# Two head groups of attention values share one PSUM bank, in a one-core transformer layer

## The reference

```
q, k, v = x @ Wq, x @ Wk, x @ Wv              # 16 heads of 8 dimensions; rotary on q and k
attn = softmax(causal(q @ k.T / sqrt(8)))
x = layernorm(x + (attn @ v) @ Wo)
logits = x @ router_w.T + experts_bias        # 8 experts, the best two of a row, softmax of the two
x = layernorm(x + sum_e cw[e] * ffn_e(x) + shared_ffn(x))   # ffn: (silu(x w1) * (x w3)) w2, hidden 256
```

## Time and profile before

| what | us |
|---|---|
| median of 3 runs | 580.99 |
| lowest and highest | 580.41, 583.55 |
| the profiled execution, from first to last instruction | 604.0 |
| TensorE busy in it | 530.3 (88%) |
| VectorE busy | 487.5 (81%) |
| ScalarE busy | 314.4 (52%) |
| GpSimd busy | 309.0 (51%) |

### The profile page before, as it was taken

The page is one execution under the profiler, slowest core; times in us unless marked ns, Lnnn a source line. Parts: engine busy times, 40 slices in busy tenths (PEclk is TensorE's granted clock), DMA queues, the critical chain, the costliest instruction groups (busy, mean ns, idle before and its releaser), DMA issues.

```text
span 604.0 us, 14723 instructions
## 1 busy us (share of the span) xinstructions
PE 530.3 (88%) x4350; PEld 350.6 (58%) x4350; DVE 487.5 (81%) x1981; ACT 314.4 (52%) x744; POOL 309.0 (51%) x517
## 2 busy tenths in 40 slices
PE   6868997988999999999999999999994997999941
PEld 3312354534665656656666777666873996885531
DVE  4797799978999899899899879879951766768883
ACT  3107665646766566667676555776660444532200
POOL 5216546566364466657873556547584324143531
PEclk9777799989999989999999799999997999999985
DMA  6573321265426256454674374643464499960111
GB/s 187 143 238 100 107 81 47 88 207 170 117 73 194 82 155 179 116 165 111 195 188 123 92 237 146 187 129 111 121 186 163 121 283 269 310 219 19 52 40 35
DMA packets 75279, 87.40 MB, mean 145 GB/s; under 512 B 9984, under 2 KB 57984, under 8 KB 75200
## 3 DMA queue, kind: packets, MB, share of 16 engines
q1 hardware_dynamic: 67824, 77.21, 43.5%
q0 software_dynamic: 3584, 7.35, 4.0%
q10 hardware_dynamic: 3792, 1.90, 1.1%
HBM read 64.28 MB, written 20.05 MB: 140 GB/s over the span
## 4 chain that ended last, share of the span: by engine, by line
PE 54%; DVE 14%; issue 9%; SPq 6%; DMA 5%; ACT 4%; another core or an unknown queue 4%; POOL 2%; ACTq 0%; DVEq 0%; POOLq 0%
PE ps L1459 14%; PE ps L1365 9%; PE ps L1321 9%; PE ps L1471 7%; DVE sums L1578 3%; PE ps L1376 3%; ACT probs L1166 2%; PE ps L1443 2%; PE ps L1481 1%; DVE acc L1758 1%; DMA stack<-mparts 1%; SPq L957 1%; POOL yg L1122 1%; PE ps L1307 1%
## 5 line engine op out<-in xcount | busy, mean ns | idle before, releaser
L1578 DVE CUSTOM_DVE_ANT_0 sums<-ps,mask_sb 128x384 bf16<-128x384 f32 (+3 forms) x512 | 218.2, 484 | 18.1 <-PE ps L1321 17.7
L1166 ACT ACTIVATE probs<-ps 128x512 f32<-128x512 f32 x320 | 170.8, 611 | 48.0 <-PE ps L1321 42.5
L1100 POOL TENSOR_SCALAR_AFFINE_SELECT probs<-probs 128x256 f32<-128x256 f32 (+1 forms) x320 | 113.6, 365 | 128.4 <-ACT probs L1166 121.1
L1321 PE MATMUL ps<-stack 64*128 64x256 bf16 (+3 forms) x1024 | 116.6, 311 | 14.6 <-DMA stack<-mparts 5.1
L1459 PE MATMUL ps<-xgT,w_tile 128*128 128x128 f32 x672 | 91.8, 283 | 3.9 <-ACT xgT L1227 1.6
L1459 PEld LDWEIGHTS ps<-xgT,w_tile 128*128 128x128 f32 x672 | 82.7, 195 | 10.5 <-issue 7.6
L1365 PE MATMUL ps<-probs,va 128*32 128x512 f32 (+3 forms) x1024 | 82.6, 466 | 3.3 <-POOL probs L1100 1.7
L1710 DVE SCALAR_TENSOR_TENSOR gate<-th,ps 128x256 f32<-128x256 f32 x116 | 48.5, 418 | 43.0 <-ACT th L1233 36.9
L1321 PEld LDWEIGHTS ps<-stack 64*128 64x128 bf16 x1024 | 41.4, 95 | 70.5 <-issue 16.1
L1122 POOL DMA_INDIRECT yg<-rows_out,slot x56 | 54.0, 963 | 55.0 <-DVE acc L1758 29.9
L1233 ACT ACTIVATE th<-ps 128x256 f32<-128x256 f32 x116 | 45.3, 391 | 48.4 <-PE ps L1459 38.6
(11 more groups left out here) (119 smaller groups left out, 702.5 us busy)
## 6 DMA issues: line engine op xcount, KB each, us to landing
w_tile<-in_experts SPq DMA_DIRECT2D x92, 384.0 KB
stack<-parts_scratch SPq DMA_DIRECT2D x98, 128.0 KB
parts_scratch<-parts SPq DMA_DIRECT2D x14, 384.0 KB
xg<-rows_in SPq DMA_DIRECT2D x18, 256.0 KB
rows_out<-y_routed SPq DMA_DIRECT2D x61, 64.0 KB
rows_in<-zeros SPq DMA_DIRECT2D x14, 192.0 KB, 3.9
x_t<-in_x SPq DMA_DIRECT2D x8, 256.0 KB, 3.6
x_r<-in_x SPq DMA_DIRECT2D x8, 256.0 KB
```

The source lines that it names most:

```text
L1100: pool.affine_select(out=area, in_=area, compare_op=ALU.is_ge, fill=0.0, base=0, pattern=pattern, channel_multiplier=-1).then_inc(masked, 1)
L1166: act.activation(probs[:, (s * NB + v) % PRING, :], bank("scores", s, v), ACT.Exp, scale=SCALE)\
L1321: return pe.matmul(into[:, at:at + width], here[:, stationary, at_s:at_s + P], here[:, moving, at_m:at_m + width], start=True, stop=True)
L1578: ins = dve.tensor_tensor_reduce(sums[:, use % 2, at:at + w], bank("max", s, u)[:, at:at + w], mask_sb[:, S - w:S], -1.0, 3.0e38, ALU.add, ...
```

## The change

- The value groups 0 and 1 accumulate into one bank, and so do 2 and 3. The stationary operand `va` now holds for each pair of heads 48 columns: head one in columns 0 to 8, zeros, head two in columns 32 to 40, zeros. The first group's matmuls read columns 0 to 31, the second's columns 16 to 47, so that in the 32 output rows of a slot head one lands in rows 0 to 8 and head two in rows 16 to 24. The accumulation is started by the first group and ended by the second. The number and the shapes of the value matmuls stay.
- ScalarE copies two banks of a sequence into `ot` instead of four; two transpositions for a row tile instead of four; the results of two row tiles fit one bank, so a call of `heads_transposes` claims one bank instead of two.
- `normalize` does one reciprocal of 32 columns and one product of 256 columns for a call, instead of two of each with half the columns.
- The first group of a pair signals a semaphore of its own (`values_read`), on which the exponentials that reuse its `probs` units wait; the columns of Wv and the rows of Wo are permuted on the host.
- `COST` of the two `heads_T` pieces is changed, a kind `values_out` is added for ACT, and all of `LATER` is replaced.

```diff
-    pe=dict(... heads_T=(890, 1060),
+    pe=dict(... heads_T=(450, 620),
-    dve=dict(... heads_T=(803, 910),
+    dve=dict(... heads_T=(560, 660),
+        for h in range(GROUPS // 2):
+            add(now + AT["values"] + UPG * (2 * h + 2), "values_out", s, h)
+        if kind == "values":
+            both = (key[0], key[1] // 2)
+            return [] if key[1] % 2 else [((kind, *both), (engine, reader, *both))]
-        if kind in ("project", "heads_T", "dense_gate"):
+        if kind in ("project", "dense_gate"):
...
+        def weighed(s, g):
+            return filled("values", s, g // 2) if g % 2 else (values_read, GROUPS // 2 * s + g // 2 + 1)
...
-            pool.memset(va[:, :, :, DK:DK + 1], 1.0).then_inc(setup_p, 1)
+            for side in range(2):
+                ins = pool.memset(va[:, :, :, 32 * side + DK:32 * side + DK + 1], 1.0)
+            ins.then_inc(setup_p, 1)
...
-            def values_out(s, g):
-                act.wait_ge(*filled("values", s, g))
-                if g == 0 and s > 0:
-                    act.wait_ge(*filled("heads_T", s - 1, 1, 1))
-                act.activation(ot[:, g, :], bank("values", s, g), ACT.Copy).then_inc(free("values", s, g), 1)
+            def values_out(s, h):
+                act.wait_ge(*filled("values", s, h))
+                if h == 0 and s > 0:
+                    act.wait_ge(*filled("heads_T", s - 1, 1))
+                act.activation(ot[:, h, :], bank("values", s, h), ACT.Copy).then_inc(free("values", s, h), 1)
...
-                take("values", s, g)
+                into, second = bank("values", s, g // 2), g % 2
+                if not second:
+                    take("values", s, g // 2)
...
-                        last = pe.matmul(bank("values", s, g)[32 * k:32 * k + 32, j * P:S], va[:, j, PER_PV * g + k, :],
-                                         probs[:, (s * NB + v) % PRING, at:at + S - j * P], start=(j == 0), stop=(j == T - 1),
-                                         skip_group_check=True)
-                last.then_inc(full("values", s, g), 1)
+                        last = pe.matmul(into[32 * k:32 * k + 32, j * P:S],
+                                         va[:, j, PER_PV * (g // 2) + k, 16 * second:16 * second + 32],
+                                         probs[:, (s * NB + v) % PRING, at:at + S - j * P],
+                                         start=(j == 0 and not second), stop=(j == T - 1 and second == 1), skip_group_check=True)
+                last.then_inc(full("values", s, g // 2) if second else values_read, 1)
...
+                take("heads_T", s, pair)
                 for n in range(2):
                     t = 2 * pair + n
-                    take("heads_T", s, pair, n)
-                    for g in range(GROUPS):
-                        last = pe.transpose(bank("heads_T", s, pair, n)[:, g * P:(g + 1) * P], ot[:, g, t * P:(t + 1) * P], ident_sb[:, :])
-                    last.then_inc(full("heads_T", s, pair, n), 1)
+                    for h in range(GROUPS // 2):
+                        at = (2 * n + h) * P
+                        last = pe.transpose(bank("heads_T", s, pair)[:, at:at + P], ot[:, h, t * P:(t + 1) * P], ident_sb[:, :])
+                last.then_inc(full("heads_T", s, pair), 1)
...
+                dve.wait_ge(*filled("heads_T", s, pair))
+                oq = bank("heads_T", s, pair).rearrange("p (u c) -> p u c", c=16)
+                inverse = rden[:, 2 * pair:2 * pair + 2, :].rearrange("p t h -> p (t h)")
+                link(dve.reciprocal(inverse, oq[:, :, DK]), rden_done, 2 * s + pair + 1)
+                dve.tensor_tensor(on[:, 2 * pair:2 * pair + 2, :].rearrange("p t (h d) -> p (t h) d", d=DK), oq[:, :, 0:DK],
+                                  inverse.rearrange("p (u o) -> p u o", o=1).broadcast_to([P, 2 * H, DK]),
+                                  ALU.mult).then_inc(free("heads_T", s, pair), 1)
```

Of `LATER` two of its 79 entries, before and after:

```diff
-         ("act", "values"): (-268.17, -117.23, -81.25, 129.78, -56.72, -170.37, -619.73, -885.2, -558.27, -432.32,
-         -110.15, -277.99),
+         ("act", "values_out"): (-2105.76, -1787.93, -1697.56, -583.3, -3888.91, -4689.17, -4349.28, -3516.7, -4293.05,
+         -3093.81, -2874.72, -2037.86),
-         ("pe", "heads_T"): (-709.01, -718.43, -476.07, -268.98, -111.31, -392.14, -837.02, -647.44, -498.38, -598.34,
-         -471.24, -468.92),
+         ("pe", "heads_T"): (-1263.31, -3006.95, -367.24, -2843.55, -1026.06, -1809.9, -3302.95, -2934.64, -1691.2,
+         -763.6, -1651.08, -1775.85),
```

More of the change, by code:

```diff
@@ L422, in build_block @@
               "count": ("dve", "count"), "rank": ("dve", "rank"), "gate": ("dve", "glu"), "project": ("dve", "project"),
-              "heads_T": ("dve", "heads_T"), "score_pair": ("act", "scores"), "max_pair": ("dve", "max"),
+              "heads_T": ("dve", "heads_T"), "values": ("act", "values_out"), "score_pair": ("act", "scores"), "max_pair": ("dve", "max"),
               "dense_gate": ("dve", "dense_glu"), "dense_down": ("dve", "mix"), "dense_end": ("dve", "mix_end")}
@@ L493, in needs @@
             if kind == "heads_T":
-                return [("act", "values", s, GROUPS - 1), ("pe", "out_T", s - 1, 0), ("pe", "heads_T", s, 0) if key[1] else None]
+                return [("act", "values_out", s, GROUPS // 2 - 1), ("pe", "out_T", s - 1, 0), ("pe", "heads_T", s, 0) if key[1] else None]
             if kind == "out_T":
@@ L547, in needs @@
                 return [("dve", "router", s, 0)]
+            if kind == "values_out":
+                return [("pe", "values", s, 2 * key[1] + 1)] + ([("pe", "heads_T", s - 1, 1)] if key[1] == 0 else [])
             if kind == "tanh":
@@ L1193, in store_v @@
                 if s > 0:
-                    act.wait_ge(*filled("values", s - 1, GROUPS - 1))
+                    act.wait_ge(*weighed(s - 1, GROUPS - 1))
                 else:
@@ L1271, in _ @@
                     store_v(key[0])
-                elif kind == "values":
+                elif kind == "values_out":
                     values_out(*key)
@@ L1594, in normalize @@
             def normalize(s, pair):
-                for n in range(2):
-                    dve.wait_ge(*filled("heads_T", s, pair, n))
-                    oq = bank("heads_T", s, pair, n).rearrange("p (h c) -> p h c", c=32)
-                    ins = dve.reciprocal(rden[:, 2 * pair + n, :], oq[:, :, DK])
-                link(ins, rden_done, 2 * s + pair + 1)
-                for n in range(2):
-                    t = 2 * pair + n
-                    oq = bank("heads_T", s, pair, n).rearrange("p (h c) -> p h c", c=32)
-                    dve.tensor_tensor(on[:, t, :].rearrange("p (h d) -> p h d", d=DK), oq[:, :, 0:DK],
-                                      rden[:, t, :].rearrange("p (h o) -> p h o", o=1).broadcast_to([P, H, DK]),
-                                      ALU.mult).then_inc(free("heads_T", s, pair, n), 1)
+                dve.wait_ge(*filled("heads_T", s, pair))
[5 more added lines that the diff above has]
+                                  ALU.mult).then_inc(free("heads_T", s, pair), 1)
             def layernorm_stats(n, rows, src, st, m, ve, chain, var_sem):
```

314 lines of the change are left out of this document (163 added, 151 removed).

## The result

The change made the kernel slower: 592.88 us median (587.70 to 595.64, 4 runs) against 580.85 us (580.41 to 583.55, 4 runs), ratio 1.0185 with a 95% interval of 1.0138 to 1.0231, that is +10.7 us (8.0 to 13.4). I had said 573.0, range 561 to 588. One run of e12, in the chip's slower state, is left out of its ratio.

What follows compares the result with a forecast made beforehand. The prediction took TensorE as the bound from 50 to 450 us, VectorE second. Its terms, -6.9 - 0.4 + 2.2 - 2.9 = -8.0 us, took the median from 580.99 to 573.0 us, range 561 to 588.

Steps and rivals of the forecast that it cites:

- What bounds the kernel: From 150 to 450 us TensorE is 97% busy, VectorE 89%; TensorE's time counts nearly in full, VectorE's in part.
- Transpositions, -6.9: On TensorE, 64 fewer transpositions of the heads at 0.107 us each save 6.9 us.
- Value matmuls and copies, 0: Value matmuls keep number and shapes; 16 fewer ScalarE copies free 9.6 us of busy time; both taken as 0.
- VectorE, -0.4: Normalization saves 2.9 us of VectorE's busy time, worth 0.4 us by its 14% share of the chain.
- Banks, +2.2: Value banks held longer raise TensorE's 4.5 us of waits for VectorE's bank releases by half, costing 2.2 us.
- The rival: Held value banks make score and maxima pairs wait: +12.3 us, 586.0; chance 0.17, shared with an order opening idle time.
- The new order, -2.9: New queue order closes an eighth of TensorE's 23.0 us idle between 50 and 450 us, saving 2.9 us.
- The signs I had named: Trace marks: 64 transpositions, 16 copies, VectorE's two groups near 11.5 us, TensorE busy near 523 us, middle stage shorter.
- TensorE under 95% in the middle: TensorE's busy share from 150 to 450 us falling below 95%, as the sign that the gain is hidden.
- a hidden gain: Rival: VectorE's row maxima set the pace and TensorE only waits more; 581.5 us, range 578 to 584, chance 0.17.
- Idle before the score matmuls released by VectorE of well over 4.5 us: TensorE's idle time before score and maxima matmuls, ended by VectorE's release, as the sign of held banks.

Runs made afterwards that it cites:

- e12: Kernel before with each reciprocal and product of VectorE's normalization issued once more, into an unused tile; 590.40 us, ratio 1.0131.
- e8: Kernel before with each of the 128 transpositions of the heads issued twice; 595.25 us, ratio 1.0190.
- e1: Kernel before, unchanged, run again for a second trace; ratio 1.0000, span 582.4 us.
- e10: The changed kernel, run again against the kernel before; 595.98 us, ratio 1.0214.
- e5: Kernel before, same order; only the planner's bank dealing changed, reserving each even value group's bank until the odd group's copy; 599.60 us, ratio 1.0270.
- e4: Kernel before with ScalarE's copy of each even value group moved right ahead of the odd group's copy; 599.34 us, ratio 1.0266.
- e7: Kernel before in its own order, with seven of the eight PSUM banks in use throughout; 611.05 us, ratio 1.0448.
- e2: Changed kernel with every queue in the order of the kernel before, banks dealt out anew; 593.26 us, ratio 1.0164.
- e3: Kernel before with every queue in the changed kernel's order, two copies where that has one; 596.61 us, ratio 1.0244.
- e9: Changed from kernel before: each value group keeps its own bank, VectorE adds odd to even groups before half as many transpositions; 582.53 us, ratio 1.0002.

## Why the prediction was wrong

*What bounds the kernel.* Right for TensorE, too low for VectorE. Its share of the chain, 14%, was read as the worth of its time. Per us of busy time e12 gives 0.84, at the place that the change touches, with the later results in it. A chain names one engine at each moment, also where two are nearly level, as at the 97% and 89% of the middle stage.

*Transpositions, -6.9.* Right mechanism, size a little over: 5.6 (4.3 to 6.8) by e8. A record takes 277 ns in e1 and 281 ns after. e8 shows that this duration isn't the price, which is a third of it. The Trainium skill (TensorE: Matmul & The Clock Gate, Part 4: PE-mode transpose) gives about 275 ns for one in one kernel's context. As a duration the traces agree with that.

*Value matmuls and copies, 0.* Mean 453 ns against 466 before, but 469 in e10, so nothing is seen. Copies weren't isolated. The 9.1 us for which TensorE waited for the last of them belonged to the untypical execution, as said above.

*VectorE, -0.4.* The two groups are at 12.4 us against 15.0 and 14.7 in e1, so 2.3 us less busy time, not 2.9: the reciprocal of 32 columns takes 353 ns, where I took 290. At 0.84, taken from the same place, it is worth -1.9.

*Banks, +2.2. This is the step that failed.* Measured, the hold costs +15.8 us (e5, interval 12.8 to 18.8) and +15.5 (e4). The step has +2.2 us and the runs show 15.8 in its place. The mechanism, its place and its length (21.6 us more in the sequence of the earlier trace rows) were right. The rival had priced it at 12.3 and put the outcome at 586.0, with its range up to 596; the change landed there, and I gave it 0.17. That its price came near is partly luck, for the quarter of an upper end that made it was a choice that no row gave. The error was in what I took for the size: the 4.5 us of idle time that the profile puts down to VectorE's releases, increased by half. That row can't show what a bank is worth. In e5 and e7 15.1 of 18.8 and 19.2 of 26.8 us of the longer spans are TensorE's busy time, as lost overlap and in part as a lower clock; in e7 the idle row is at 6.6 us with 26 us lost.

*The new order, -2.9.* I had called it a choice that no row forces, and it has no support: changed kernel and e2 differ by 2 to 5 thousandths, to the side of slower. In the traces the starts of a pair's two groups lie 159 us apart in sum over the changed kernel and 208 us over e2, so the new order does shorten the hold by a quarter, and what it wins there it loses elsewhere; where wasn't isolated.

*Sum by the measured terms* for the structure in the old order: +15.8 - 5.6 - 1.9 = +8.3 us. e2 measured +9.6 (7.2 to 12.0). The account closes within its uncertainty, with nothing needed for copies, value matmuls or the banks of the transposed heads that are given back. For the new order the same terms with e3's +14.2 give +6.7, against 10.7 (8.0 to 13.4) and, in e10, 12.4 (9.2 to 15.8); there it closes only at the edge of the intervals.

*The signs I had named.* 64 transpositions at "some 9.5 us" (10.2), 16 copies, value matmuls unchanged: as said. VectorE's two groups came to 12.4, not 11.5. TensorE's busy time came to 525.7, not 523, and the 523 started from the untypical trace: e1 has 524.8, so it didn't fall at all. The middle stage had fewer instructions rather than a shorter stretch. "TensorE under 95% in the middle", my mark of a hidden gain, was just missed, at 95.1%. "Idle before the score matmuls released by VectorE of well over 4.5 us" was named as the mark of held banks: it came to 5.6 us, and the loss was there all the same. That mark was wrong.

## What to carry to other kernels

In a kernel like this one, whose PSUM banks are dealt out piece by piece, count bank-microseconds as a resource like engine time: price what an edit holds, not just what it issues, and price it by taking a bank away and timing it, not from the idle time put down to releases. Here short waits showed as lost overlap; compare counts of instructions in equal windows, or a group's busy time at an unchanged mean. An engine's share of the chain wasn't the worth of its time: at 97% and 89% both engines counted, and in e9 the work shifted from one to the other gained nothing. When a run adds work to price an engine, put it where nobody waits for what stands behind it, or the price holds lateness too.

## What the runs showed of the hardware

A whole bank of eight was worth 26.2 us (4.5%) here (e7), and about 200 us of holding, spread over 16 stretches, was worth 15.8 (e5). Kernels that held both pairs in the old order ran at a mean granted clock of 0.935 where the kernel before had 0.943 to 0.945. A further 128x128 fp32 transposition costs 0.067 to 0.106 us in a busy TensorE while its record says 277 ns. The spread between executions of one kernel was 578.9 to 588.7 us for before and 587.7 to 598.4 us for the changed kernel, and one profiled execution of before spanned 604.0 us, with 11.3 us in one pause of ScalarE. The cause of that pause wasn't tried.
